# A count by target block: the comparison of 56 tiles laid out with eight tiles innermost

## The chip, the cores and the metric

The kernel runs on one NeuronCore of a Trainium2 chip. The metric is the device time of one execution in microseconds (us). Its engines: TensorE (PE; PEld is its weight load), VectorE (DVE), ScalarE (ACT), GpSimd (POOL, which here prepares the indirect DMAs) and SyncE (SP, which issues the plain DMAs).

## The reference

Two graph layers over 50,000 nodes with 256 features and 50,000 edges:

```
h = relu(layernorm(x))
x = x + relu(segment_sum(h[dst] @ W0[edge_type], src) + bias)     # rows gathered by dst, added by src
h = relu(layernorm(x))
y = h @ W_neigh; keep the 32 largest of each row of y
x = x + h @ W_self + segment_sum(y[src], dst) / max(degree(dst), 1)
```

The kernel orders the edges on the chip: by type for layer 0, by their target `dst` for layer 1. For that it counts, for every tile of 128 edges and every block of 128 target nodes, how many edges of the tile fall into the block. The change is in this count.

## The kernel before

**Layer 0** works through 100 batches (`NBT`) of four tiles (`B` = 4) of 128 edge slots. Each batch b passes these stations, each on its own engine:

- POOL, `gather_and_add`: for each of the four tiles it issues a gather of the rows of x for batch b + 3 (L655) and then an add of the messages of batch b into `agg` in HBM (L667). Each of these is an indirect DMA that POOL has to prepare itself. A gather waits for the normalised rows (h) of an earlier batch, an add for its message and for the add two before it.
- DVE, `edge0_front`: compares keys (L923, L930, L931), copies the index of a later gather (L940, which first waits until the gather of this batch has landed), takes the statistics (L899, L903) and scales. Then `edge0_cross` (L950) and `edge0_back` of the batch before.
- ACT: normalises h (L1217), copies `hT` (L1230) and the messages (L1235) out of the banks.
- PE, `edge0_body`: fold (L1416), product (L1474, L1485) and degree (L1424) for each of the four tiles.
- SP loads the key rows of a batch (L534) once the cross comparison of an earlier one is done.

**The sort by target** is cut into chunks that ride along: `edge0_body` of DVE and PE runs over 101 steps, divided by `PHASES` (L473): "hist" with `HSTEPS` = 13 steps, "rank" with 30, "sort" with 56, "rest" with the 2 that are left. Each step does one batch and, behind it, one chunk.

- In "hist", `hist_hots` (L968) builds for a chunk of `HC` = 49 tiles two tables of f16 zeros and ones: `high_hot` (L971: the number of the target's group, `high16`, against 0 to 97, 49 x 98 comparisons per partition) and `low_hot` (L973: `low16` against 0 to 3). PE's `hist_count` (L1439) multiplies them, one small matmul per tile with `high_hot` (128 x 98) as the weights and `low_hot` (128 x 4) moving. `hist_evict` (L979) copies the result two steps later. There are `HCHUNKS` = 8 chunks, in steps 0 to 7; step 10 forms sums (`bucket_sums`) and step 12, the last, the starts (`bucket_starts`).
- "rank" and "sort" (L1014 to L1022, L1046 to L1054, L1462) need what "hist" has counted.

The order on each engine is the order in the code. `zone_c` is a piece of SBUF that many of these tables share: `high_hot` at its start, `low_hot` behind it, from `RANK` on the tables of "rank", from `DEGREES` on those of the degree count. Before the batches, DVE casts the number tables `iota_f` and `iota_h` from `iota_i` (L786, L787), and a first stage (L839 to L854) orders the slots by type. After them come the node stage, the tables of layer 1 and its merge.

Of the kernel before, what the change touches and what calls it, by code (L numbers as in the profile page):

```python
# [21 lines left out]
F16 = mybir.dt.float16  # L22
U16 = mybir.dt.uint16
I32 = mybir.dt.int32
ALU = mybir.AluOpType
ACT = mybir.ActivationFunctionType

P = 128
# [26 lines left out]
HI = 98  # L55
LO = 4
# [67 lines left out]
def wait_from(eng, sem, value, batch, first):  # L124

    if not isinstance(batch, int) or batch >= first:
        eng.wait_ge(sem, value)
# [18 lines left out]
def graph_layers(nc, x, src, dst, etype, w_rel, bias, w_self, w_neigh, out):  # L146
# [7 lines left out]
    with ctx:  # L154
        def sb(name, shape, dt=F32):
            return ctx.enter_context(nc.sbuf_tensor(name, shape, dt))
# [8 lines left out]
        bank = [banks[:, i, :] for i in range(8)]  # L165
# [3 lines left out]
        iota_h = sb("iota_h", [P, COLS], F16)  # L169
# [21 lines left out]
        zone_c = sb("zone_c", [P, 11 * B * D])  # L191

        def view(zone, at, shape, dt=F32):

            size = 1
            for n in shape:
                size *= n
            words = size if dt in (F32, I32) else size // 2
            flat = zone[:, at:at + words]
            if dt != F32:  # L200
                flat = flat.bitcast(dt)
            if len(shape) == 2:
                return flat.rearrange("p (a b) -> p a b", a=shape[0])
            if len(shape) == 3:
                return flat.rearrange("p (a b c) -> p a b c", a=shape[0], b=shape[1])
            return flat

        iota_i = view(zone_a, 0, [STEPS1], I32)
# [20 lines left out]
        high16 = sb("high16", [P, COLS], F16)  # L229
# [16 lines left out]
        def two(name, shape, dt=F32):  # L246
            return [sb(f"{name}{p}", shape, dt) for p in range(2)]

        def two_views(zone, at, shape, dt=F32):
            words = 1  # L250
            for n in shape:
                words *= n
            words = words if dt in (F32, I32) else words // 2
            return [view(zone, at + p * words, shape, dt) for p in range(2)]

        rows_in = two("rows_in", [P, B, D])
        h = two("h", [P, B, D])
# [37 lines left out]
        fields4 = two("fields4", [P, B, FIELDS])  # L295


        HC, HCHUNKS, HSTEPS = 49, 8, 13
        counts = view(zone_a, 0, [LO, TILES])
        sums = view(zone_a, LO * TILES, [LO, TILES])  # L300
        starts_i = view(zone_b, 0, [LO, TILES], I32)
        starts16 = view(zone_b, LO * TILES, [TILES, 2 * LO], F16)
        high_hot = two_views(zone_c, 0, [HC, HI], F16)
        low_hot = two_views(zone_c, HC * HI, [HC, LO], F16)
        total4 = sb("total4", [P, LO])
        rowsum = sb("rowsum", [P, 1])
        base = sb("base", [P, 1])
# [6 lines left out]


        RC, RCHUNKS = 14, 28
        RANK = HC * (HI + LO)
        DEGREES = RANK + 2 * RC * P + RC * LO
        one_low = two_views(zone_c, DEGREES, [B, P], F16)
        one_high = two_views(zone_c, DEGREES + B * P, [B, TILES], F16)  # L320
        bucket_in = two_views(zone_c, RANK, [RC * P], F16)
        high_in = two_views(zone_c, RANK + RC * P, [RC * P], F16)
        low_pick = two_views(zone_c, RANK + 2 * RC * P, [RC, LO], F16)
        rank_junk = view(zone_a, 0, [RC, P], F16)
# [137 lines left out]
        DEG, SORT = 2, 6  # L462
# [310 lines left out]
        def _(dve):  # L773
            count = [0]

            def link(ins):

                count[0] += 1
                ins.then_inc(own, 1)
                dve.wait_ge(own, count[0])  # L780

            v = nc.vector
# [2 lines left out]
            dve.wait_ge(consts, 3)  # L785
            v.tensor_copy(iota_f[:, :], iota_i[:, :])  # L786
            v.tensor_copy(iota_h[:, :], iota_i[:, 0:COLS])  # L787
            link(v.tensor_copy(part_f[:, :], part_i[:, :]))
            for c in range(LO):
                v.tensor_scalar(part98[:, c:c + 1], part_f[:, :], float(HI * c), None, ALU.add)  # L790
# [11 lines left out]
            for r in range(R):  # L802
                last = v.tensor_scalar(masks[:, r, :], tab["type"][:, 0:TILES], float(r), None, ALU.is_equal, ALU.add,
                                       accum_out=tot[:, r:r + 1])
# [163 lines left out]
            def hist_hots(c, p):  # L968
                wait_from(dve, histmm, c - 1, c, 2)
                at = slice(c * HC, (c + 1) * HC)  # L970
                v.tensor_tensor(high_hot[p], iota_h[:, 0:HI].unsqueeze(1).to_broadcast([P, HC, HI]),  # L971
                                high16[:, at].unsqueeze(2).to_broadcast([P, HC, HI]), ALU.is_equal)
                v.tensor_tensor(low_hot[p], iota_h[:, 0:LO].unsqueeze(1).to_broadcast([P, HC, LO]),  # L973
                                low16[:, at].unsqueeze(2).to_broadcast([P, HC, LO]), ALU.is_equal
                                ).then_inc(hist_hot, 1)
# [82 lines left out]
            def edge0_body(phase, at, chunk):  # L1058
                for part, lag in ((edge0_front, 0), (edge0_cross, 1), (edge0_back, 1)):
                    b, r, p = at.back(lag)  # L1060
                    if inside(b, NBT):
                        part(b, r, p)
                c, rc, pc = chunk.back(0)
                e, re, _ = chunk.back(2)
                if phase == "hist":
                    if c < HCHUNKS:
                        hist_hots(c, pc)
                    if 0 <= e < HCHUNKS:
                        hist_evict(e, pc)
                    if e == HCHUNKS:  # L1070
                        bucket_sums()
                    if c == HSTEPS - 1:
                        bucket_starts()
                if phase == "rank":
                    if inside(e, RCHUNKS):
                        rank_out(e, re, pc)
                    if inside(c, RCHUNKS):
                        rank_hots(c, rc, pc)
                if phase == "sort":
                    if isinstance(c, int) and c == 0:  # L1080
                        dve.wait_ge(rank_own, 4 * RCHUNKS)
                        slots_of_positions()
                    sort_hots(c, rc, pc)
# [284 lines left out]
        def _(pe):  # L1368
            mm = nc.tensor.matmul
# [4 lines left out]
            for k, n in enumerate(NAMES):  # L1374
                for c in range(COLS // P):
                    last = nc.tensor.transpose(bank[k][:, c * P:(c + 1) * P], rawf[n][:, c, :], ident[:, :])
# [18 lines left out]
            for c in range(COLS // P):  # L1395
                last = nc.tensor.transpose(bank[4][:, c * P:(c + 1) * P], key0[:, c * P:(c + 1) * P], ident[:, :])
# [33 lines left out]
            def half(j, n):  # L1430

                return range((2 * j - B) * n // B, (2 * j - B + 2) * n // B)

            def hist_count(c, p, j):
                if j == B // 2:
                    pe.wait_ge(hist_hot, c + 1)
                    wait_from(pe, hist_out, c - 1, c, 2)
                for t in half(j, HC):
                    last = mm(bank[SORT + p][0:HI, t * LO:(t + 1) * LO], high_hot[p][:, t, :], low_hot[p][:, t, :],  # L1439
                              start=True, stop=True)  # L1440
                if j == B - 1:
                    last.then_inc(histmm, 1)
# [76 lines left out]
            for k in range(2):  # L1519
                for c in range(LO):  # L1520
                    last = mm(bank[SORT + k][:, 0:TILES], ones[0:HI, 0:P], passed_nodes[0:HI, c, k * TILES:(k + 1) * TILES],
                              start=(c == 0), stop=(c == LO - 1))
# [29 lines left out]
            for k in range(2):  # L1552
                for c in range(LO):
                    last = mm(bank[SORT + k][:, 0:TILES], dstT[0:HI, c, :], tile_hot[0:HI, c, k * TILES:(k + 1) * TILES],
                              start=(c == 0), stop=(c == LO - 1))
# [5 lines left out]
            def merge_steps(i, half):  # L1561
                _, words = nc.values_load_multi_w_load_instructions(
                    fetch[0:1, bass.ds(i * 2 + half, 1), :].rearrange("o g w -> o (g w)"),
                    engines=[mybir.EngineType.PE], min_val=0, max_val=(RING - 1) * D,
                    skip_runtime_bounds_check_because="the table holds ring offsets, bounded by the ring")
                for k in range(GROUP):
                    s, at = i * (2 * GROUP) + (half * GROUP + k), half * GROUP + k
                    if k % FETCHED == 0:
                        pe.wait_ge(arrived, nc.s_assert_within(words[GROUP + k // FETCHED], 1, TILES + RING))
                    if k % PAIR == 0:  # L1570
                        pe.wait_ge(hot1_done, i * (2 * GROUP // PAIR) + (at // PAIR + 1))
                    if s >= 8:
                        pe.wait_ge(summed, s - 7)
                    mm(bank[at % 8][:, 0:D], hot1[:, at % HOTS, :], ring_cols[:, bass.ds(words[k], D)],  # L1574
                       start=True, stop=True).then_inc(steps1, 1)
# [26 lines left out]
```

## Time and profile before

| | |
|---|---|
| median of 3 runs | 3427.87 us (3419.07 to 3433.84) |
| profiled execution | 3424.89 us |
| its span, first to last instruction | 3423.2 us |
| mean granted TensorE clock, as a share of 2.4 GHz | 0.912 |
| DVE busy | 3036.0 us (89%) |
| PE busy | 2528.3 us (74%) |
| POOL busy | 2461.4 us (72%) |
| ACT busy | 2198.9 us (64%) |

How to read it: a busy share is a mean over stages with different limits, and a stage is bound by the engine that never waits in it. The histogram stage lies at 303 to some 500 us, the rank chunks go on to about 930 us, the sort chunks to 1675 us. In the views, an operation is named by engine and line, with what it writes and reads; a number in square brackets is the idle time of the engine before it and what ended that. Idle time put down to "issue" is time for which the profile shows no wait.

### The profile page before, as it was taken

Reading aid. Unit: us, or ns where it says so; the run is one execution under the profiler, and the core shown is the slowest. Engines: PE = TensorE matmul, PEld = TensorE weight load, DVE = VectorE, ACT = ScalarE, POOL = GpSimd, SP = SyncE. Lnnn points to the kernel's source line nnn. Section 1 sums busy time; section 2 is a strip of 40 time slices with the busy share of each in tenths; the row PEclk is TensorE's granted clock in tenths of the full one; section 3 lists DMA queues with packets and bytes.
Section 4 is the critical chain, followed back from the end, with each engine's and each line's share of the span. In section 5 each row is a group of like instructions: output and inputs, shape, how many; then the busy total and the mean of one; then the engine's idle time right before and its main releaser. Section 6 shows DMA issues by size and latency. Waiting matters only on the chain.

```text
span 3423.2 us, 64727 instructions
## 1 busy us (share of the span) xinstructions
PE 2528.3 (74%) x10740; PEld 1658.5 (48%) x10741; DVE 3036.0 (89%) x13368; ACT 2198.9 (64%) x6002; POOL 2461.4 (72%) x1732
## 2 busy tenths in 40 slices
PE   3665766767788888888777777777777775777787
PEld 1224655555566666666533333333333333565565
DVE  8999778888899999999789999999999997777777
ACT  5994233323333333333379999999999995777776
POOL 0004886767788888888678888888888885777775
PEclk8998888888899999999989999999999998999989
DMA  9702466666655555555544545445455453889897
GB/s 364 285 0 52 80 116 150 144 139 152 127 105 106 103 106 103 106 103 106 84 155 175 194 173 189 178 173 194 172 186 181 174 190 145 295 285 303 285 306 252
DMA packets 308089, 576.91 MB, mean 169 GB/s; under 512 B 32095, under 2 KB 188034, under 8 KB 307982
## 3 DMA queue, kind: packets, MB, share of 16 engines
q1 hardware_dynamic: 212366, 419.40, 35.9%
q0 software_dynamic: 95616, 156.31, 23.5%
q8 instruction: 40, 0.66, 0.1%
q14 instruction: 67, 0.55, 0.0%
HBM read 316.70 MB, written 258.88 MB: 168 GB/s over the span
## 4 chain that ended last, share of the span: by engine, by line
DVE 45%; issue 24%; PE 15%; DMA 7%; POOL 5%; DVEq 2%; ACT 1%; POOLq 1%; ACTq 0%; SPq 0%
DVE best L1165 6%; DVE w L1172 6%; DVE zone_c L1172 6%; PE banks L1574 5%; DMA agg<-msg,sidx 4%; PE banks L1474 4%; DMA w<-hs,gidx 2%; POOL w L734 2%; PE banks L1416 2%; DVE zone_c L846 2%; DVE zone_c L1050 2%; DVE zone_c L1054 2%; DVE zone_c L848 2%; DVE zone_c L1200 2%; DVE zone_c L1052 2%
## 5 line engine op out<-in xcount | busy, mean ns | idle before, releaser
L1546 PE MATMUL banks<-w,hT 128*128 128x512 f32 x1568 | 764.5, 645 | 252.2 <-ACT hT L1326 247.7
L667 POOL DMA_INDIRECT agg<-msg,sidx x400 | 667.1, 1668 | 185.2 <-issue 123.0
L655 POOL DMA_INDIRECT rows_in<-in_x,gidx x400 | 433.4, 1084 | 414.9 <-DVE gidx L871 280.5
L1546 PEld LDWEIGHTS banks<-w,hT 128*128 128x128 f32 x1568 | 312.8, 204 | 646.0 <-issue 508.7
L1200 DVE SCALAR_TENSOR_TENSOR zone_c<-banks,rdeg,zone_c 128x256 f32 x784 | 379.3, 484 | 158.6 <-PE banks L1574 123.1
L1574 PE MATMUL banks<-w,zone_c 128*128 x1568 | 405.5, 417 | 143.2 <-POOLq L742 113.8
L1416 PE MATMUL banks<-pick,h 128*128 128x128 f32 x1600 | 286.3, 307 | 301.1 <-ACT h L1217 206.1
L1474 PE MATMUL banks<-w,hT 128*128 x1600 | 482.7, 430 | 16.5 <-issue 15.1
L1235 ACT COPY msg<-banks 128x256 f32<-128x256 f32 x400 | 148.2, 370 | 510.9 <-PE banks L1485 486.5
L734 POOL DMA_INDIRECT w<-hs,gidx x392 | 372.5, 950 | 143.5 <-issue 93.8
L1416 PEld LDWEIGHTS banks<-pick,h 128*128 128x128 f32 x1600 | 256.1, 214 | 365.2 <-issue 343.1
L1574 PEld LDWEIGHTS banks<-w,zone_c 128*128 128x128 f32 x1568 | 311.5, 207 | 237.5 <-issue 188.3
L1165 DVE MAX8 best<-zone_c 128x8 f32<-128x256 f32 x980 | 341.7, 416 | 9.3 <-ACT zone_c L1319 9.3
L711 POOL TENSOR_TENSOR zone_c<-msg,zone_c 128x1024 f32<-128x1024 f32 x98 | 231.8, 2365 | 149.5 <-ACT zone_c L1312 149.5
L1474 PEld LDWEIGHTS banks<-w,hT 128*128 128x128 f32 x1600 | 309.2, 215 | 62.1 <-issue 30.9
L1172 DVE MATCH_REPLACE8 zone_c<-best,zone_c 128x256 f32<-128x256 f32 x784 | 313.3, 416 | 0.0
L700 POOL TENSOR_SCALAR zone_c<-zone_c 128x1024 f32<-128x1024 f32 x98 | 272.0, 2776 | 7.9 <-DMA zone_c<-agg 7.8
L1354 ACT ACTIVATE zone_c<-zone_c,ones 128x256 f32<-128x256 f32 x392 | 195.2, 498 | 127.4 <-PE banks L1574 126.5
L1347 ACT ACTIVATE zone_c<-iota_f,minus_key 128x128 f32<-128x128 f32 x784 | 265.6, 386 | 4.6 <-DMA hs<-zone_c 4.6
L1485 PE MATMUL banks<-msg,cross 128*128 128x256 f32 x798 | 262.7, 414 | 0.0
L1223 ACT ACTIVATE std<-mv,eps 128x4 f32<-128x4 f32 x100 | 29.7, 297 | 335.0 <-DVE mv L903 335.0
L705 POOL TENSOR_TENSOR zone_c<-rows_in,zone_c 128x1024 f32<-128x1024 f32 x98 | 233.6, 2384 | 8.6 <-POOL zone_c L700 0.2
(229 smaller groups left out, 5793.9 us busy)
## 6 DMA issues: line engine op xcount, KB each, us to landing
out_rows<-zone_c SPq DMA_DIRECT2D x196, 512.0 KB, 2.7
agg<-bias SPq DMA_DIRECT2D x2, 25344.0 KB, 97.4
zone_c<-agg SPq DMA_DIRECT2D x98, 512.0 KB, 6.1
hs<-zone_c SPq DMA_DIRECT2D x98, 512.0 KB, 3.6
zone_c<-out_rows SPq DMA_DIRECT2D x98, 512.0 KB, 5.9
rows_in<-in_x SPq DMA_DIRECT2D x97, 512.0 KB, 5.4
keyrow<-key_rows SPq DMA_DIRECT2D x100, 320.0 KB, 3.9
zone_c<-bucket_rows SPq DMA_DIRECT2D x28, 448.0 KB
```

Source lines behind the costliest of these rows:

```text
L655: pool.indirect_dma_start(out=rows_in[p][:, j, :], out_offset=None, in_=x[:, :], in_offset=bass.IndirectOffsetOnAxis(ap=gidx[p][:, j:j + 1 ...
L667: pool.indirect_dma_start(out=agg[:, :], out_offset=bass.IndirectOffsetOnAxis(ap=sidx[p][:, j:j + 1], axis=0), in_=msg[p][:, j * D:(j + 1) ...
L700: nc.gpsimd.tensor_scalar_max(agg_in[p][:, :, :], agg_in[p][:, :, :], 0.0).then_inc(relu_n, 1)
L734: pool.indirect_dma_start(out=ring[:, k, :], out_offset=None, in_=hs[:, :], in_offset=bass.IndirectOffsetOnAxis(ap=gidx1[p][:, k:k + 1], a ...
L1165: last = v.max(best[:, j, :], (work if k else neigh)[p][:, j, :])
L1172: last = v.match_replace(work[p][:, j, :], best[:, j, :], (work if k else neigh)[p][:, j, :], NEG)
L1200: ins = v.scalar_tensor_tensor(to, bank[at % 8][:, 0:D], rdeg[:, bass.ds(node, 1)], to, ALU.mult, ALU.add)
L1347: last = nc.scalar.activation(near[:, k % NEARS, j * P:(j + 1) * P], iota_f[:, 0:P], ACT.Abs, bias=minus_key[:, bass.ds(q * PAIR + j, 1)])
L1416: last = mm(bank[j // 2][:, k * P:(k + 1) * P], h[p][:, j, c * P:(c + 1) * P], pick[p][j][:, 0:P], start=True, stop=True)
L1474: last = mm(to, hT[p][:, j // 2, k * P:(k + 1) * P], w0[:, bass.ds(rel, 1), c, :].rearrange("k r d -> k (r d)"), start=(c == 0), stop=alon ...
L1546: last = mm(bank[4 + j][:, :], hT[p][:, c, j * P:(j + 1) * P], w1[:, c, :], start=(c == 0), stop=(c == KC - 1))
L1574: mm(bank[at % 8][:, 0:D], hot1[:, at % HOTS, :], ring_cols[:, bass.ds(words[k], D)], start=True, stop=True).then_inc(steps1, 1)
```

## The change

`hist_hots` compares 56 tiles per call in place of 49, so there are 7 chunks and 12 "hist" steps in place of 8 and 13; one more step falls to "rest". The table `high_hot` is laid out as [7, 98, 8]: eight tiles innermost. For that a new table `iota_w` holds each number 0 to 97 eight times; it is cast once from `iota_i`. The weights of a tile's matmul are then 98 f16 values at a step of 8 elements (16 bytes). `low_hot` keeps its layout, with 56 tiles, and has two tiles of its own outside `zone_c`. `RANK`, and `DEGREES` with it, move.

```diff
-        HC, HCHUNKS, HSTEPS = 49, 8, 13
+        HC, HCHUNKS, HSTEPS, HW = 56, 7, 12, 8
...
-        high_hot = two_views(zone_c, 0, [HC, HI], F16)
-        low_hot = two_views(zone_c, HC * HI, [HC, LO], F16)
+        high_hot = [t.rearrange("p a (h w) -> p a h w", w=HW)
+                    for t in two_views(zone_c, 0, [HC // HW, HI * HW], F16)]
+        low_hot = [t[:, :, :] for t in two("low_hot", [P, HC, LO], F16)]
+        iota_w = sb("iota_w", [P, HI, HW], F16)
...
-        RANK = HC * (HI + LO)
+        RANK = HC * HI
...
             v.tensor_copy(iota_h[:, :], iota_i[:, 0:COLS])
+            v.tensor_copy(iota_w[:, :, :], iota_i[:, 0:HI].unsqueeze(2).to_broadcast([P, HI, HW]))
...
-                v.tensor_tensor(high_hot[p], iota_h[:, 0:HI].unsqueeze(1).to_broadcast([P, HC, HI]),
-                                high16[:, at].unsqueeze(2).to_broadcast([P, HC, HI]), ALU.is_equal)
+                v.tensor_tensor(high_hot[p], iota_w[:, :, :].unsqueeze(1).to_broadcast([P, HC // HW, HI, HW]),
+                                high16[:, at].rearrange("p (a w) -> p a w", w=HW).unsqueeze(2).to_broadcast(
+                                    [P, HC // HW, HI, HW]), ALU.is_equal)
...
-                    last = mm(bank[SORT + p][0:HI, t * LO:(t + 1) * LO], high_hot[p][:, t, :], low_hot[p][:, t, :],
+                    last = mm(bank[SORT + p][0:HI, t * LO:(t + 1) * LO], high_hot[p][:, t // HW, :, t % HW],
+                              low_hot[p][:, t, :],
                               start=True, stop=True)
```

## Rows read from the trace of the kernel before

**Rows 1.** The page: busy time of each engine; the chain that ended last.

```profile
PE 2528.3 (74%) x10740; PEld 1658.5 (48%) x10741; DVE 3036.0 (89%) x13368; ACT 2198.9 (64%) x6002; POOL 2461.4 (72%) x1732
DVE 45%; issue 24%; PE 15%; DMA 7%; POOL 5%; DVEq 2%; ACT 1%; POOLq 1%; ACTq 0%; SPq 0%
```

**Rows 2.** Busy time by windows: stretch, length, engines (instructions), granted clock, DMA share, GB/s.

```profile
343.00:430.00 87.00, 61.26 (x465) 53.02 (x465) 63.96 (x231) 24.04 (x56) 74.81 (x41) 0.79 0.45 79
430.00:482.00 52.00, 37.76 (x182) 31.31 (x182) 36.19 (x188) 20.59 (x48) 42.25 (x33) 0.89 0.60 107
```

**Rows 3.** The line L971: duration in ns least/median/most, first and last start.

```profile
L971 DVE TENSOR_TENSOR zone_c<-iota_h,high x8: 5152/5152/5154, 303.0 to 411.6; 128x4802 f16<-128x4802 f16 x8
```

**Rows 4.** Timeline of POOL and DVE, one steady step: start us, duration us, operation.

```profile
358.76 5.15 DVE L971 TENSOR_TENSOR zone_c<-iota_h,high 128x4802 f16<-128x4802 f16 x1
359.25 6.12 POOL L667 DMA_INDIRECT agg<-msg,sidx  x1 [0.30 <-issue]
...
365.67 1.11 POOL L655 DMA_INDIRECT rows_in<-in_x,gidx  x1 [0.30 <-ACT msg L1235]
...
369.14 1.00 POOL L655 DMA_INDIRECT rows_in<-in_x,gidx  x1 [0.30 <-issue]
...
371.99 0.17 DVE L940 COPY gidx<-from 128x4 int32<-128x4 int32 x1 [3.95 <-DMA rows_in<-in_x,gidx]
...
376.34 5.15 DVE L971 TENSOR_TENSOR zone_c<-iota_h,high 128x4802 f16<-128x4802 f16 x1
```

**Rows 5.** Timeline of POOL: held calls, and two calls one plain step apart.

```profile
317.51 4.64 POOL L655 DMA_INDIRECT rows_in<-in_x,gidx  x1 [4.66 <-ACT h L1217]
...
344.14 5.02 POOL L655 DMA_INDIRECT rows_in<-in_x,gidx  x1 [0.30 <-issue]
...
412.01 6.19 POOL L667 DMA_INDIRECT agg<-msg,sidx  x1 [0.30 <-issue]
...
431.54 1.00 POOL L655 DMA_INDIRECT rows_in<-in_x,gidx  x1 [0.30 <-ACT msg L1235]
...
444.34 1.00 POOL L655 DMA_INDIRECT rows_in<-in_x,gidx  x1 [0.30 <-issue]
```

**Rows 6.** Timeline of DVE: two one-input f16 comparisons, and a cast.

```profile
310.70 0.24 DVE L930 TENSOR_SCALAR zone_c<-iota_h,lowcol 128x128 f16<-128x128 f16 x1
310.86 0.31 DVE L931 TENSOR_SCALAR zone_c<-iota_h,highcol 128x392 f16<-128x392 f16 x1
...
6.60 0.57 DVE L786 CAST iota_f<-zone_a 128x784 f32<-128x784 int32 x1 [6.60 <-POOL zone_a L651]
```

**Rows 7.** The chain through PE in one step; a weight load's row of the page.

```profile
376.95 1.20 PE banks L1416 x4
...
384.58 1.06 PE banks L1439 x24
...
388.76 5.79 issue
...
L1416 PEld LDWEIGHTS banks<-pick,h 128*128 128x128 f32 x1600 | 256.1, 214 | 365.2 <-issue 343.1
```

**Rows 8.** Timeline of ACT and POOL: the first message of batch 4, and its add.

```profile
380.64 0.37 ACT L1235 COPY msg<-banks 128x256 f32<-128x256 f32 x1 [3.05 <-PE banks L1485]
...
391.22 1.58 POOL L667 DMA_INDIRECT agg<-msg,sidx  x1 [0.30 <-issue]
```

**Rows 9.** Timeline of DVE, POOL, and the chain, at the end of layer 0.

```profile
1670.48 0.17 DVE L1046 COPY fields<-fields 128x28 f32<-128x28 f32 x1
...
1675.52 0.15 DVE L916 COPY lowcol<-low 128x4 f32<-128x4 f32 x1
...
1678.90 0.16 DVE L940 COPY gidx<-from 128x4 int32<-128x4 int32 x1
...
1672.20 1.00 POOL L655 DMA_INDIRECT rows_in<-in_x,gidx  x1 [0.30 <-issue]
...
1683.85 0.82 PE banks L1416 x4
```

## The prediction

> **What bounds the kernel now.** I read the page first: DVE is busy for 89% of the span, POOL for 72%, and the chain that ended last is 45% DVE [rows 1]. Read alone, that says "shorten any DVE work and win it all". The stage has to be asked instead, so I went to busy time by windows around the calls of L971. In the stretch with the last five of the eight (343 to 430 us) DVE is busy 63.96 of 87 us, 74%, and POOL 74.81, 86%; in the plain steps after them (430 to 482) DVE falls to 36.19 of 52 us [rows 2]. So here DVE is not full. The timeline of the two engines side by side tells why. L971 starts at 358.76 and lasts 5.15 us. POOL's next call, an L667 that starts at 359.25, lasts 6.12 us, where the same call elsewhere lasts 1.58 [rows 4, 8]: POOL is held until DVE's comparison ends (363.91) and then does its own work. DVE in turn reaches L940 and sits idle 3.95 us for the gather that POOL issued at 369.14. From one L971 to the next it is 17.58 us [rows 4]. A plain step of POOL, with no comparison in it, goes from 431.54 to 444.34, 12.80 us [rows 5]; its only gaps there are the 0.30 us between calls. So **from 317.5 us on POOL's queue is the bound of the histogram stage**, and one comparison costs it 6.12 - 1.58 = 4.54 us in the steady steps. POOL calls of 4.64, 5.02 and 6.19 us stand in chunks 1, 3 and 7; each chunk has one such call [rows 5].
>
> **The comparison.** Now 49 x 98 = 4802 elements per call take 5152 ns [rows 3], eight calls. With a fixed part of about 0.15 us (L940, with four elements, takes 0.17 us [rows 4]) that is 1.04 ns an element: one per tick. One input, high16, has step 0 innermost. After the change all three operands run with step 1 over eight f16 innermost, 56 x 98 = 5488 elements, seven calls. The total stays 392 x 98, so without a faster rate there is nothing to gain. What rate? The trace has no f16 operation with two such input streams, so I bound it. Above: 1.04 ns, as now, 5488 x 1.04 + 0.15 = 5.87 us. Below: the one-input f16 comparisons of L930 and L931, where 264 elements more cost 0.07 us [rows 6], 0.27 ns each, would give 1.6 us. Two inputs carry twice the data of one, so I take half the rate of the one-input form, 0.53 ns; the cast of L786 shows a rate of that size too (784 elements in 0.57 us) [rows 6]. That gives **5488 x 0.52 + 0.15 = 3.0 us a call, 2.15 us less than 5.15**.
>
> The Trainium skill, VectorE: DVE Perf Modes, "The perf-mode tier table", says that tensor_tensor on 16-bit data in SBUF with step 1 makes two elements a cycle, never four; by its 1224 ns for 2048 elements a call would be about 3.0 us, an estimate. No row here shows that form.
>
> **What of it lies on the path.** The hold on POOL ends with the call, so each call that is 2.15 us shorter holds POOL 2.15 us less, whatever DVE then does with its time:
> - chunk 0: here POOL was not yet full; it waits 4.66 us for h before 317.51 [rows 5], and h waits for DVE, which is behind the comparison. DVE is 2.15 us earlier: 2.15.
> - chunks 1 to 6: 6 x 2.15 = 12.9.
> - chunk 7: there is none any more; its hold of 6.19 - 1.58 = 4.61 goes [rows 5, 8].
> Sum 19.7 us. The eighth histogram step becomes one more step of the last phase, so the 101 steps stay; POOL issues the same gathers and adds. What is late next: a step is then 12.8 + (4.54 - 2.15) + 0.3 = 15.4 us, with POOL still the bound; DVE's own work in it is 17.58 - 3.95 - 2.15 = 11.5 us, PE's about 12.1 (below). The keyrow load, issued behind the cross comparison of a step, lost 2.15 us of cover, but DVE has 3.9 us of idle time in the same step to pay for it.
>
> **PE.** The weights of L1439 were 98 adjacent f16 and are now 98 at a step of 16 bytes. Now a pair of load and matmul goes every 1.06/24 = 44 ns; PE works from 376.95 to 388.76, 11.8 us, and is then idle 5.79 us [rows 7]. With 56 pairs in place of 49 it is 12.1 us. A step has room until 15.4, that is 3.3/56 = 59 ns more a pair; behind that come some 8 us that the message lies ready before POOL adds it: 380.64 against 391.22 [rows 8], 10.6 us, less the 2.15 that POOL gains. No row has weights with a stride. Bounds: no cost, and the 214 ns at which the profile books the slowest weight loads (L1416) [rows 7], 170 ns more than now. I take a pitch up to twice 44 ns, which is hidden.
>
> The Trainium skill, SBUF — State Buffer, "Door 1: The DMA port swizzle", says that SBUF has lines of 16 bytes and that each access that crosses to a new one pays. With this layout every weight lies in a line of its own; the page gives no price for TensorE, and none is used here. It is the rule that speaks against the change (second rival).
>
> **Smaller terms.** The table iota_w is one cast of 784 elements on DVE before the first transposes, on the path: L786, of the same size, takes 0.57 us [rows 6]; with the step-0 input at one element per tick it would be 0.9. I take +0.5. The low comparison and the eviction grow from 196 to 224 elements and lose one call: nothing. The move of one step to the end: now DVE ends its last sort chunk before the front of batch 99, whose L940 comes at 1678.90, behind 5.04 us of chunk work (1670.48 to 1675.52), although the last gather was issued at 1672.20 and, by the 2.85 us from issue to L940 in the steady steps, was there at 1675.05 [rows 4, 9]. With a plain step before it DVE has no chunk there and waits for the gather only. The fold of 1683.85 comes up to 3.85 us earlier, and the last adds hang on it [rows 9]. I take -3.5; bounds 0 and -3.9. The new addresses in zone_c and the two tiles of low_hot: nothing, bounds -3 and +3 by the spread of such things in the rank phase; no row shows it.
>
> **Sum**: -2.15 - 12.9 - 4.6 - 3.5 + 0.5 = **-22.6 us**. Against the profiled execution (3424.89 us, span 3423.2) that is 3402.3; the median of the three runs stands 3.0 us above that execution, and from 3427.87 it is **3405**. The steps behind (rank, sort, nodes, merge) are unchanged and start earlier. The three runs before reach from 3419 to 3434, so about 0.5%, 17 us, is what a measurement of this kernel can tell from no change; the forecast of 0.66% lies not far above it.
>
> **Rivals.**
> 1. *The form stays at one element a tick* (the broadcast in the middle, or is_equal with two inputs, takes no faster mode). For: no row shows such a rate for two inputs. Against: comparisons with one input do run packed [rows 6]. Then a call is 5.87 us, 0.72 longer: 7 x 0.72 - 4.6 - 3.5 + 0.5 = -2.6, **3425**: no change. Chance 0.14.
> 2. *PE becomes the bound through the strided weights*, at L1439. For: the stride, and that pairs follow at 44 ns, near to nothing but the load. Against: 5.79 us idle per step and 8 us of messages in stock. With d ns more a pair the loss is 7 x (56 d - 3.3) - 8 us: nothing up to d = 80 ns, the whole gain at 7 x (56 d - 3.3) = 30.6, d = 137 ns (a pitch of 180, four times now); from there it is slower than before. At 214 ns (d = 170) the loss is 7 x 6.2 - 8 = 35.5, **3441**; slower by over 0.5% from d of about 180 ns. Chance 0.14: 0.03 that it costs little, 0.07 within 0.5%, 0.04 slower.
> 3. *The forecast's mechanism with other sizes* belongs to the forecast: 3397 if a call reaches 1.6 us or the address terms help; 3414 if the end gives nothing and a hold is less regular.
>
> **How the numbers follow.** Forecast 0.72, of which 0.60 lies below 3410.7 (faster by over 0.5%) and 0.12 above; rival 1 0.14 (within); rival 2 0.14 as split. Faster 0.63, same 0.33, slower 0.04. The range 3396 to 3426 takes in the forecast with the bounds of its terms and rival 1, and leaves out the upper half of rival 2 and what scatter remains.
>
> **What would show it.** L971: 7 calls near 3.0 us (5.9 refutes). POOL calls under it of about 4.0 us in place of 6.12; L971 to L971 15.4 us; L940 still idle for the gather. PE: the pitch of L1439 under 100 ns and idle time left at the end of each step; if PE has none and POOL waits for msg, rival 2 holds. L940 of batch 99 waiting for its gather. If POOL shows waits on its own adds in these steps, or the rank phase (30 steps) gets longer or shorter, my sum is wrong in a place I did not price.

## The result, and the profile after

The changed kernel takes **3452.54 us** (median of 5 runs, 3451.58 to 3460.62) against 3427.89 us before: ratio **1.0081, 95% interval 1.006 to 1.0102**. The forecast was 3405 us. The profiled execution has a span of 3450.6 us, 27.4 us more than before.

Where the 27.4 us are is read from four lines in each kernel: the comparison, the first operation of the rank chunks, the last comparison of the sort chunks, and the reciprocal that ends layer 0. Each row gives duration in ns least/median/most, then first and last start in us. Before (its comparison stands in [rows 3]):

```profile
L1014 DVE TENSOR_SCALAR zone_a<-zone_c,part_f x28: 678/686/908, 501.9 to 905.4; 98x1792 f16<-98x1792 f16 x28
L1054 DVE TENSOR_SCALAR zone_c<-iota_h,fields x392: 303/314/587, 947.5 to 1675.3; 128x392 f16<-128x392 f16 x196
L1095 DVE RECIPROCAL rdeg<-rdeg x1: 2603/2603/2603, 1710.3 to 1710.3; 128x392 f32<-128x392 f32 x1
```

After:

```profile
L974 DVE TENSOR_TENSOR zone_c<-iota_w,high x7: 3004/3009/3011, 304.4 to 417.0; 128x5488 f16<-128x5488 f16 x7
L1018 DVE TENSOR_SCALAR zone_a<-zone_c,part_f x28: 672/686/912, 518.8 to 921.6; 98x1792 f16<-98x1792 f16 x28
L1058 DVE TENSOR_SCALAR zone_c<-iota_h,fields x392: 303/313/519, 962.8 to 1697.0; 128x392 f16<-128x392 f16 x196
L1099 DVE RECIPROCAL rdeg<-rdeg x1: 2603/2603/2603, 1743.2 to 1743.2; 128x392 f32<-128x392 f32 x1
```

| stretch | before, us | after, us | difference |
|---|---|---|---|
| up to the first comparison | 303.0 | 304.4 | +1.4 |
| histogram: first comparison to first rank operation | 198.9 | 214.4 | +15.5 |
| rank and sort chunks | 1173.4 | 1178.2 | +4.8 |
| last sort chunk to the end of layer 0 | 35.0 | 46.2 | +11.2 |
| node stage and merge | 1712.9 | 1707.4 | -5.5 |

The comparison is what was forecast: 3.009 us for 3.0. Yet the histogram stretch, which has one step less (12.8 us) and by the forecast 19.7 us of shorter holds, should have come to 198.9 - 12.8 - 19.7 = 166.4 us and is 48 us above that. The busy time by windows shows which engine took it (columns: stretch, its length, busy time and instructions of PE, PEld, DVE, ACT and POOL, granted clock, DMA share, GB/s):

```profile
343.00:430.00 87.00, 87.00 (x405) 79.08 (x405) 42.88 (x184) 19.74 (x44) 49.80 (x32) 0.70 0.36 64
```

PE is busy for all of the 87 us, where it was 61.26 [rows 2]; DVE falls from 63.96 to 42.88 us and POOL from 74.81 to 49.80. The chain through PE in one step (start, duration, what), against [rows 7]:

```profile
371.88 0.17 PE banks L1428
372.04 4.88 PE banks L1443 x28
376.92 1.07 PE banks L1420 x4
377.99 1.71 PE banks L1479 x4
379.69 0.85 PE banks L1490 x2
380.55 0.33 PE banks L1428
380.87 4.85 PE banks L1443 x28
```

Before, 24 pairs of load and matmul took 1.06 us, 44 ns each, and PE then sat idle for 5.79 us. Now 28 pairs take 4.88 us, **174 ns each**, and nothing is idle. POOL waits for the message, which ACT copies out when PE has it. ACT's statistics for DVE (L1227) stand behind that copy, and DVE waits for them:

```profile
368.18 1.58 POOL L669 DMA_INDIRECT agg<-msg,sidx  x1 [5.93 <-ACT msg L1239]
...
371.91 0.37 ACT L1239 COPY msg<-banks 128x256 f32<-128x256 f32 x1 [1.53 <-PE banks L1490]
372.18 0.30 ACT L1227 ACTIVATE std<-mv,eps 128x4 f32<-128x4 f32 x1
...
372.51 0.18 DVE L911 RECIPROCAL rstd<-std 128x4 f32<-128x4 f32 x1 [10.11 <-ACT std L1227]
```

### The profile page after: what moved, and what is told of

Same layout as the page of the kernel before. It is cut to its first block, busy times and chain, and to the rows that moved or that the text cites. A ratio compares the mean times of both kernels' runs of the same rounds, so it can differ in the third digit from the quotient of the medians.

```text
span 3450.6 us, 64689 instructions
## 1 busy us (share of the span) xinstructions
PE 2589.4 (75%) x10740; PEld 1713.9 (50%) x10741; DVE 3025.6 (88%) x13366; ACT 2200.7 (64%) x6002; POOL 2433.3 (71%) x1732
## 4 chain that ended last, share of the span: by engine, by line
DVE 45%; issue 22%; PE 15%; DMA 8%; POOL 5%; DVEq 3%; ACT 1%; POOLq 1%; ACTq 0%; SPq 0%
DVE best L1169 6%; DVE zone_c L1176 6%; DVE w L1176 6%; DMA agg<-msg,sidx 5%; PE banks L1579 4%; PE banks L1479 3%; POOL w L736 3%; DMA w<-hs,gidx 3%; DVE zone_c L849 2%; PE banks L1420 2%; DVE stats L902 2%; DVE zone_c L851 2%; DVE zone_c L1054 2%; PE banks L1443 2%; DVE zone_c L1056 2%
## 5 line engine op out<-in xcount | busy, mean ns | idle before, releaser
L669 POOL DMA_INDIRECT agg<-msg,sidx x400 | 657.4, 1644 | 245.3 <-issue 124.9
L657 POOL DMA_INDIRECT rows_in<-in_x,gidx x400 | 414.3, 1036 | 416.6 <-DVE gidx L874 281.1
L1394 PE MATMUL banks<-zone_c 128*128 128x400 f16 x784 | 150.6, 336 | 114.3 <-ACT zone_c L1268 88.4
```

The lines of the kernel that those rows point to most:

```text
L657: pool.indirect_dma_start(out=rows_in[p][:, j, :], out_offset=None, in_=x[:, :], in_offset=bass.IndirectOffsetOnAxis(ap=gidx[p][:, j:j + 1 ...
L669: pool.indirect_dma_start(out=agg[:, :], out_offset=bass.IndirectOffsetOnAxis(ap=sidx[p][:, j:j + 1], axis=0), in_=msg[p][:, j * D:(j + 1) ...
```

## The experiments

Theory A: the strided weight loads make PE the bound of the histogram steps, and all that DVE and POOL gained lies under it. Rival B: the loss comes from the new chunks, the moved step or the new addresses. Rival C: DVE and its hold on POOL still set the time. Ratios are to the kernel before on the same chip. Four kernels (2, 4 and 14 innermost, and each pair twice) ran on a chip on which the kernel before takes 3534 us; where an expectation names microseconds, their ratio is taken times 3428. "Histogram" and "end" in the text below are the stretches of the table above, read in the same way; a table of all kernels stands behind the last experiment.

**Chunks alone.** The layout and the comparison of before in the new chunks:

```diff
-        high_hot = [t.rearrange("p a (h w) -> p a h w", w=HW)
-                    for t in two_views(zone_c, 0, [HC // HW, HI * HW], F16)]
+        high_hot = two_views(zone_c, 0, [HC, HI], F16)
...
+                v.tensor_tensor(high_hot[p], iota_h[:, 0:HI].unsqueeze(1).to_broadcast([P, HC, HI]),
+                                high16[:, at].unsqueeze(2).to_broadcast([P, HC, HI]), ALU.is_equal)
...
-                    last = mm(bank[SORT + p][0:HI, t * LO:(t + 1) * LO], high_hot[p][:, t // HW, :, t % HW],
+                    last = mm(bank[SORT + p][0:HI, t * LO:(t + 1) * LO], high_hot[p][:, t, :],
```

> The changed kernel with the layout and the comparison of before: 56 tiles a chunk, 7 chunks, 12 steps, low_hot in its own tiles, but weights contiguous and no number table. Theory A (the strided weight loads make PE the bound of the histogram steps): the comparison takes 5.87 us, the pair of load and matmul 44 ns, POOL is the bound again, and the time is about 3425 us, within 0.3% of before. Rival B (the loss comes from the chunking: seven larger chunks, one step moved from the histogram phase to the end, new addresses): about 3452 us, like the changed kernel.

Measured: 3427.11 us, ratio 1.000 (0.9989 to 1.001). The comparison takes 5.87 us. So the chunks, the moved step and the addresses cost nothing beyond the 0.1% that the measurement can tell: rival B falls.

**Number table with a step of 0.** The strided layout, without the eight copies:

```diff
-                v.tensor_tensor(high_hot[p], iota_w[:, :, :].unsqueeze(1).to_broadcast([P, HC // HW, HI, HW]),
+                v.tensor_tensor(high_hot[p], iota_h[:, 0:HI].unsqueeze(1).unsqueeze(3).to_broadcast([P, HC // HW, HI, HW]),
```

> The changed kernel without the table of eight copies: the number comes from the plain table with a step of 0 innermost, the layout and the strided weights stay. The comparison should go back to one element a tick, 5.87 us. Theory A: PE is the bound in these steps, so the slower comparison costs nothing: 3449 to 3457 us, and the step from comparison to comparison stays at 21 to 22 us. Rival C (DVE and its hold on POOL still set the time of these steps): seven comparisons longer by 2.86 us each, 20 us more, about 3472 us.

Measured: 3456.86 us, ratio 1.0086 (1.0063 to 1.0109). The comparison is back at one element a tick, 5867 ns in place of 3009 (its line, as above):

```profile
L974 DVE TENSOR_TENSOR zone_c<-iota_h,high x7: 5860/5867/5870, 304.0 to 419.0; 128x5488 f16<-128x5488 f16 x7
```

That is seven times 2.86 us more on DVE, and POOL's held calls get longer with it (5.36 and 4.95 us between 319 and 340 us, where the changed kernel has 2.50 and 3.34). Yet the histogram is only 2.6 us longer (217.0 against 214.4). The intervals of the two ratios (changed kernel and this one) overlap; with the 20 us of rival C the ratio would be 1.014, outside. Rival C falls: in the changed kernel the fast comparison is worth next to nothing, since PE is behind it.

**Fast comparison with contiguous weights.** `high16` is held twice per tile instead, so both inputs and the output run with step 1 over two elements, and the table stays tile by tile:

```diff
+        high2 = sb("high2", [P, COLS, 2], F16)
...
+            link(v.tensor_copy(high2[:, :, :], code16_i.unsqueeze(2).to_broadcast([P, COLS, 2])))
...
+                v.tensor_tensor(high_hot[p].rearrange("p t (g w) -> p t g w", w=2),
+                                iota_h[:, 0:HI].rearrange("p (g w) -> p g w", w=2).unsqueeze(1).to_broadcast(
+                                    [P, HC, HI // 2, 2]),
+                                high2[:, at, :].unsqueeze(2).to_broadcast([P, HC, HI // 2, 2]), ALU.is_equal)
```

> Fast comparison and contiguous weights together: high16 is held twice for each tile (a pair of equal values), so that both inputs and the output run with step 1 over two elements, and the table stays tile by tile. 56 tiles a chunk as in the changed kernel. Theory A: comparison 3.0 us, pair 44 ns, POOL the bound with holds of about 2.4 us; the forecast of the prediction for this form, about 3405 us (3400 to 3412). Rival B (chunking): at least 3440 us. Rival D (a fast comparison gives nothing because POOL's hold does not shrink with it): about 3425 us.

Measured: **3401.89 us, ratio 0.9928 (0.9906 to 0.9949)**. It beats both kernels. The comparison and POOL's call under it, from its timeline, against [rows 4]; and PE's idle time at the end of the step, from its chain:

```profile
368.66 3.01 DVE L971 TENSOR_TENSOR zone_c<-iota_h,high 128x5488 f16<-128x5488 f16 x1
...
369.01 4.11 POOL L667 DMA_INDIRECT agg<-msg,sidx  x1 [0.30 <-issue]
...
379.64 0.17 DVE L940 COPY gidx<-from 128x4 int32<-128x4 int32 x1 [3.84 <-DMA rows_in<-in_x,gidx]
...
383.99 3.01 DVE L971 TENSOR_TENSOR zone_c<-iota_h,high 128x5488 f16<-128x5488 f16 x1
```

```profile
380.34 1.24 PE banks L1441 x28
381.58 3.02 issue
```

POOL's call takes 4.11 us where it took 6.12 (1.58 of its own and a hold of 2.53 in place of 4.54), the step 383.99 - 368.66 = 15.3 us (forecast 15.4), POOL is the bound, PE idle 3.0 us. Rival D falls with the hold. This is the forecast's mechanism as written, with contiguous weights in place of strided ones. The total fits it better than the parts do: the span is 22.3 us shorter (forecast 22.6), but layer 0 ends only 17.5 us earlier, and the other 4.8 us lie behind it, where the code is that of before.

**The pairs alone, in the chunks of before.** `HC, HCHUNKS, HSTEPS = 49, 8, 13` in the kernel above.

> The kernel before with nothing but the fast comparison by pairs: 49 tiles a chunk, 8 chunks, 13 steps, contiguous weights. The comparison should take 4802 x 0.52 + 0.15 = 2.65 us, 2.5 us less, eight times. If POOL's hold gives that back, ratio to before 0.994 (20 us less), of which the kernel with pairs and 56 tiles (ratio 0.9928) has some 3 us more by its moved step. If the chunking carried the gain, the ratio is 1.000.

Measured: 3404.66 us, ratio 0.9933 (0.9915 to 0.995). Comparison 2.652 us; histogram 179.1 us, 19.8 less than before; end 33.5. Eight times 2.50 us is 20.0: each microsecond off the comparison comes back as one. The 3 us more that the moved step was expected to give the kernel with 56 tiles cannot be seen: 0.9933 against 0.9928 is within the intervals.

**The step of the weights.** `HW` = 2, 4 or 14 in place of 8; the comparison takes 3.01 us in all of them.

> The changed kernel with two tiles innermost in place of eight (each number held twice): weights at a step of 4 bytes. Theory L (a weight load pays about 1.75 ns for each new line of 16 bytes it touches, so 4 values a line are 0.44 ns each, as fast as adjacent ones): pair 44 ns, comparison 3.0 us, total 3400 to 3408 us, like the kernel with pairs. Theory S (any step but 1 takes the slow path): pair 173 ns, total about 3452 us.

> Four tiles innermost: weights at a step of 8 bytes, two values a line. Theory L: 0.87 ns a value, a pair of about 87 ns, 43 ns more than contiguous: 2.4 us more PE work a step, which its idle time holds, so 3400 to 3412 us. Theory S: 173 ns, about 3452 us. If the full price only comes with the last step to 16 bytes, the pair stays at 44 ns.

> Fourteen tiles innermost: weights at a step of 28 bytes. Theory L: every value still is in one line of its own, as at 16 bytes: pair 173 ns, about 3452 us. If the price grows with the distance, the pair is near 300 ns and the time above 3490 us.

Measured, a group of 28 pairs in the chain of each, with 2, 4 and 14 tiles innermost:

```profile
375.56 1.28 PE banks L1443 x28
```

```profile
369.63 2.46 PE banks L1443 x28
```

```profile
372.08 4.79 PE banks L1443 x28
```

That is 46, 88 and 171 ns a pair, with ratios 0.995 (0.9933 to 0.9966), 0.9967 (0.9953 to 0.9981) and 1.0078 (1.0061 to 1.0095). All three pairs are as theory L has them, and theory S falls. Of the totals only the one with 14 innermost came as expected; 0.995 is about 3411 us and 0.9967 about 3417, above the expected 3400 to 3408 and 3400 to 3412. The total of 4 tiles innermost is the one that teaches more: PE has no idle time left in its chain from 350 to 386 us, though its 2.5 us more a step should have fitted into 3.0 us of idle time, and its histogram is 173.1 us against 168.8 with two.

**Seven innermost**, a step of 14 bytes, in the chunks of before (`HC, HCHUNKS, HSTEPS, HW = 49, 8, 13, 7`).

> The changed layout in the chunking of before: 49 tiles a chunk, 8 chunks, 13 steps, seven tiles innermost, so weights at a step of 14 bytes. By the price of 1.75 ns a line of 16 bytes, 98 values touch 86 lines: a pair of 150 to 155 ns. PE's step is about 9.8 + 2.2 + 49 x 0.152 = 19.5 us against 17.6 before, eight times: ratio to before 1.003 to 1.006. If the price jumps only at a full 16 bytes, the pair is near 88 ns and the ratio 0.996.

Measured: ratio 1.0056 (1.0041 to 1.0071).

```profile
364.13 3.63 PE banks L1443 x24
```

151 ns a pair: 98 values at 14 bytes touch 85 or 86 lines, by where they start, and 86 x 1.75 = 150. The price goes by lines of 16 bytes. The ratio lies where the expected step of 19.5 us for PE had put it (the steady steps take 18.4 to 19.8 us). The comparison takes 3.01 us, not the 2.65 that the forecast's rate gives for 4802 elements (last section).

**Contiguous loads, more of them.** The kernel with pairs, with each load and matmul issued four times, and twice:

```diff
+                    for _ in range(4):
+                        last = mm(bank[SORT + p][0:HI, t * LO:(t + 1) * LO], high_hot[p][:, t, :],
+                                  low_hot[p][:, t, :],
+                                  start=True, stop=True)
```

> As the kernel with pairs, but each load and matmul of the count is issued four times (the same result written four times): PE gets about 4 x 44 = 176 ns a tile, as much as one strided pair takes in the changed kernel (4.88 us for 28), without any stride. Theory A1 (only the time that the loads hold PE counts): about 3452 us, like the changed kernel. Theory A2 (the strided loads cost more than their own time, because the granted clock falls from 1.00 to 0.50 while they run and the products behind them take 1.71 instead of 0.87 us): here the clock stays up, each step is 2 to 4 us shorter than in the changed kernel, total 3425 to 3438 us. Rival B: time does not depend on this.

> As the kernel with pairs (3402 us), but each load and matmul of the count issued twice: PE gets 56 x 44 = 2.5 us more a step if the clock stays up. By the prediction's account of PE's room (3.3 us of idle time a step and 8 us of messages in stock) this is hidden: 3400 to 3408 us. If the granted clock falls in the longer run of loads, as it did with four, a pair takes 83 ns for a part and the products behind run at half speed: PE reaches 15 to 18 us a step, 3408 to 3425 us.

Measured: with four 3492.67 us, ratio 1.0197 (1.0175 to 1.0219); with two 0.9974 (0.9964 to 0.9985). With four the time lies above what both theories expected. With two it is some 3419 us: the 3400 to 3408 that followed from PE's room missed, the 3408 to 3425 for a falling clock came. The chain with four, a longer stretch, and PE alone in the group before this one show what happened:

```profile
369.14 9.26 PE banks L1442 x112
378.40 1.06 PE banks L1418 x4
379.46 1.71 PE banks L1478 x4
```

```profile
343.00:430.00 87.00, 87.00 (x874) 80.42 (x873) 35.81 (x157) 15.17 (x34) 39.89 (x26) 0.64 0.30 53
```

```profile
358.20:360.00 1.80, 1.80 (x44) 1.00 0.53 117
360.00:362.00 2.00, 2.00 (x35) 0.68 0.71 87
362.00:363.00 1.00, 1.00 (x15) 0.50 1.05 270
```

In the group of the chain 112 pairs take 9.26 us, 83 ns each and not 44: the granted clock is down (0.64 over the stretch from 343 to 430 us; the two levels are 1.2 and 2.4 GHz) although PE is never idle there and no weight is strided. The group before it begins at the full clock and ends at half (the three lines from 358.20 on); it takes 7.04 us, 63 ns a pair. So the stride is not needed for the clock to fall; what PE did before it fell was one contiguous load after the other, each with its small matmul. With two, most groups run at the full clock (56 pairs in 2.52 us, 45 ns), but the clock is at half in the products behind some of them:

```profile
356.70:359.20 2.50, 2.50 (x58) 1.00 0.44 93
359.80:362.40 2.60, 2.60 (x8) 0.50 0.86 212
```

In the kernel with single pairs it is 1.00 over the same work (362.4 to 367.0 us). The histogram with two is 178.9 us, 10.4 more than with one; the 2.5 us more PE work a step were not hidden, against what the prediction's account of PE's room said.

**The strided loads spread out.** The changed kernel with four runs of 14 pairs a step, one chunk later, in place of two of 28:

```diff
-                for t in half(j, HC):
+                for t in range(j * HC // B, (j + 1) * HC // B):
...
-                    if j >= B // 2 and phase == "hist" and c < HCHUNKS:
-                        hist_count(c, pc, j)
+                    if phase == "hist" and 1 <= c <= HCHUNKS:
+                        hist_count(c - 1, 1 - pc, j)
```

> The changed kernel with the strided loads of a chunk spread over all four tiles of PE's next step (four runs of 14 pairs, 2.4 us each, in place of two of 28, 4.9 us). PE issues the same loads and products. If the fall of the granted clock costs a part of each step (products of a step 12.0 us where the kernel with pairs has 9.8), and shorter runs keep the clock up, a step is some 2 us shorter: 7 x 2.2 = 15 us less than the changed kernel, ratio to before 1.003 to 1.006. If only the price of the loads counts, the ratio stays at 1.008.

Measured: ratio 1.0089 (1.0059 to 1.0119), no better than the changed kernel.

```profile
368.06 2.32 PE banks L1443 x14
370.38 1.06 PE banks L1420 x4
371.44 1.71 PE banks L1479 x4
```

The products behind a run of 14 still take 1.71 us: the shorter runs did not keep the clock up. From the third comparison to the last it is 0.77 on average against 0.68 in the changed kernel, and a step there takes 20.9 us against 21.5. But the edit also moves each chunk's loads one step later: in the first 40 us of the histogram (303 to 343) PE works 32.8 us in place of 36.3, and the second step takes 23.9 us in place of 15.7. So the share of the clock in the loss could not be taken away by itself; in the next section it is worked out from the chain.

All kernels, the stretches in us, from one profiled execution each:

| kernel | comparison | pair, ns | histogram | rank and sort | end |
|---|---|---|---|---|---|
| before (13 steps) | 5.15 x 8 | 44 | 198.9 | 1173.4 | 35.0 |
| after | 3.01 x 7 | 174 | 214.4 | 1178.2 | 46.2 |
| chunks alone | 5.87 x 7 | 44 | 186.3 | 1181.0 | 44.4 |
| table with a step of 0 | 5.87 x 7 | 174 | 217.0 | 1178.7 | 45.2 |
| pairs, 56 tiles | 3.01 x 7 | 44 | 168.5 | 1175.2 | 45.6 |
| pairs, 49 tiles (13 steps) | 2.65 x 8 | 44 | 179.1 | 1184.7 | 33.5 |
| 2 innermost | 3.01 x 7 | 46 | 168.8 | 1171.1 | 44.3 |
| 4 innermost | 3.01 x 7 | 88 | 173.1 | 1173.9 | 46.4 |
| 14 innermost | 3.01 x 7 | 171 | 214.3 | 1178.9 | 45.0 |
| 7 innermost (13 steps) | 3.01 x 8 | 151 | 216.8 | 1181.6 | 35.3 |
| pairs, each twice | 3.01 x 7 | 2 x 45 | 178.9 | 1178.1 | 45.9 |
| pairs, each four times | 3.01 x 7 | 4 x 59 to 83 | 248.7 | 1182.7 | 44.7 |
| strided, spread | 3.02 x 7 | 166 to 169 | 220.0 | 1178.8 | 44.4 |

Rank and sort, whose code is the same in all, range from 1171 to 1185 us in an order that does not follow the edits; the +4.8 of the changed kernel lies within that. Its -5.5 behind layer 0 has its like in other kernels: the merge alone is 4 to 12 us shorter than before in chunks alone, the table with a step of 0, pairs with 56 tiles and each four times, whose code there is that of before. Neither is explained here.

## Why the prediction was wrong, point by point

- **The bound of the stage**, POOL and not DVE, held by DVE's comparison: right. With PE kept out of the way, eight comparisons 2.50 us shorter took 19.8 us out of the histogram (pairs, 49 tiles).
- **The comparison at two elements a tick** (a tick being the 1.04 ns that one element takes in the kernel before): right, 3.009 us for 3.0. The Trainium skill's page (VectorE: DVE Perf Modes, "The perf-mode tier table") had it, and the trace now agrees.
- **The moved step**: right in sign, wrong in mechanism. Over the kernels with 12 steps the end is 9.3 to 11.4 us longer, against the 12.8 us of the step that the histogram lost: between -3.5 and -1.4 for my -3.5, and -1.6 in the changed kernel. I had DVE wait there for nothing but the last gather. It waits for the key rows of the last batch, 2.9 to 3.3 us in all ten kernels with 12 steps, and then hardly for the gather (0.42 us at most); with no chunk of work in between, nothing covers that load. In the changed kernel:

```profile
1708.51 0.35 DVE L926 SCALAR_TENSOR_TENSOR pick<-keyrow,keycol,upto 128x128 f32<-128x128 f32 x1 [3.00 <-DMA keyrow<-key_rows]
```

- **The table's cast**: +0.5 forecast; the cast takes 0.56 us, and the first comparison came 1.4 us later.
- **PE: the step that failed.** I bounded a strided pair by 44 and 214 ns and took "a pitch up to twice 44 ns, which is hidden". It is 174 ns, near the upper bound, so PE's work in a step came to some 22 us against a room of 15.4: it was not hidden, and PE and not POOL was the bound. The rule that I set down as speaking against the change was the one to believe: The Trainium skill, SBUF — State Buffer, "Door 1: The DMA port swizzle", with its lines of 16 bytes. The runs agree that a new line costs, and add the price for weights, about 1.75 ns a line (171/98 to 174/98). They do not bear out the same passage where it has two accesses to a line, or a stride of up to 8 two-byte values, at full speed: at a step of 4 values, two to a line, a pair took 88 ns and not 44. I had given its rival 0.14.
- **And rival 2's own sum was mis-sized too.** With d = 130 ns its formula gives a loss of 7 x (56 x 0.130 - 3.3) - 8 = 20 us, so 3425 us; the histogram lost 214.4 - 168.5 = 45.9 us against contiguous weights. Two terms are at fault.
  - The 8 us of messages in stock (a reading of [rows 8], batch 4) are not there when the first chunk comes. In the kernel with pairs the first message is added 0.9 us after its copy has ended, and only from the end of batch 1 on do they lie ready for some 8 us or more. In the changed kernel POOL waits 6.6 us for its first message, at 325.75; the first message of each batch from 0 to 5 is added 0.8 or 0.9 us after its copy, and none lies longer than 3.4 us: the stock never builds. Without it the formula gives 28.
  - PE's remaining work is 9.8 us a step in the kernel with pairs (12.3 us from 369.27 to 381.58, less 2.5 of loads) and some 12 in the changed kernel (comparison to comparison 374.49 - 352.09 = 22.4 and 395.97 - 374.49 = 21.5 us, less 9.7 of loads): products behind the loads run at the lower clock, 1.71 for 0.87 us. Some 2.2 us a step, 15 in all; 28 + 15 = 43 of the 45.9 us. This share is an estimate; no run shows it by itself.

  The formula's room of 3.3 us in every step is wrong too. Four tiles innermost and the doubled loads both add 2.5 us a step, for which it gives no loss, with the stock or without; they lost 4.6 and 10.4 us against 168.5. In the kernel with pairs the first comparisons follow each other after 10.9, 11.0 and 12.2 us and only the later ones after 15.3 to 15.6: in the first steps PE has no such room. With the doubled loads POOL waits 11.3 us for messages between 318 and 440 us, 1.4 with single ones. How much of the 4.6 and 10.4 us is the first steps and how much is the clock, which falls in both kernels, stays open.

So the histogram's +45.9 us against the kernel with pairs is most of what turned a gain of 0.7% into a loss of 0.8%.

## What to carry to other kernels

A layout that is chosen for the engine that writes a table has to be priced on the engine that reads it: count the 16-byte lines that one weight load touches, and compare with the pitch of the pairs, above all where few moving columns stand behind each load. For a packed comparison against a broadcast value two equal elements innermost are enough; duplicate the broadcast operand twice, and the table's layout needs no change. Slack that one engine owes to another's lateness is not there for use: take the room of an engine as its idle time in a step, from the first step on.

## What the runs showed of the hardware that had not been expected

**A strided weight load pays by lines of 16 bytes.** 98 f16 values at steps of 2, 4, 8, 14, 16 and 28 bytes touch 13, 25, 49, 86, 98 and 98 lines: 44, 46, 88, 151, 174 and 171 ns a pair. From 49 lines on that is 1.74 to 1.80 ns a line; adjacent values do not come below 44 ns. At a step of 16 bytes the price does not follow the granted clock. In the changed kernel one run of 28 starts at the full clock and the next runs at half (columns: stretch, length, busy PE and PEld of the line L1443, granted clock, DMA, GB/s):

```profile
372.00:373.00 1.00, 1.00 (x8) 1.00 (x7) 1.00 0.19 74
...
375.00:376.00 1.00, 1.00 (x7) 1.00 (x7) 0.98 0.82 130
...
380.90:385.70 4.80, 4.80 (x27) 4.73 (x27) 0.50 0.40 69
```

The 28 pairs of the first take 4.88 us and those of the second 4.85. A contiguous pair does follow the clock, 44 against 83 ns.

**The clock fell while PE was busy without a gap**, from 1.00 to 0.50, that is from 2.4 to 1.2 GHz, in or just behind the runs of count matmuls, strided (the windows above) or contiguous (each pair four times, in the windows from 358.20 to 363.00; each twice, behind the run that ends at 359.2).

**Rows of seven cost four ticks.** With seven f16 innermost the comparison of 4802 elements takes 3.01 us, with pairs 2.65:

```profile
L974 DVE TENSOR_TENSOR zone_c<-iota_w,high x8: 3004/3010/3040, 304.1 to 424.4; 128x4802 f16<-128x4802 f16 x8
```

(3.01 - 0.15)/4802 = 0.595 ns an element is 4/7 of 1.04 ns. That fits two elements a tick with the last tick of each row half full. Rows of 2, 4, 8 and 14 ran at the full rate; whether the odd length does it, or that every other row starts at an odd element, no run separates.
